# Another prologue for a graph kernel: node table in triples of blocks, edge lists in another tile, weights awaited in parts

## What is computed

```python
edge_index = jnp.stack([src, dst])
x = _layernorm(x + gat(x, edge_index, W, att), axis=-1)      # attention over the edges, 4 heads of 32
x = _layernorm(x + gnn(x, edge_index, ...), axis=-1)         # three layers of gated message passing
# gat: xh = (x @ W).reshape(-1, H, C); alpha = leaky_relu(<xh[dst], a_i> + <xh[src], a_j>)
#      softmax of alpha over the edges of one dst; out = segment_sum(xh[src] * alpha, dst)
```

## Time and profile before

| what | us |
|---|---|
| median of 3 runs (8215.47 to 8240.46) | 8240.08 |
| the profiled execution, its time | 8238.9 |
| its span, from the first to the last instruction | 8237.1 |

### The profile page before, as it was taken

The page is one execution under the profiler, slowest core; times in us unless marked ns, Lnnn a source line. Parts: engine busy times, 40 slices in busy tenths (PEclk is TensorE's granted clock), DMA queues, the critical chain, the costliest instruction groups (busy, mean ns, idle before and its releaser), DMA issues.

```text
span 8237.1 us, 134783 instructions
## 1 busy us (share of the span) xinstructions
PE 4828.4 (59%) x26657; PEld 4110.2 (50%) x26658; DVE 4929.9 (60%) x26111; ACT 1352.1 (16%) x5266; POOL 5983.1 (73%) x6316
## 2 busy tenths in 40 slices
PE   5888888888744444444464544444446444444445
PEld 4777777777644444444454444444445444444444
DVE  7777777778755555555565555555556555555555
ACT  2333333333400000000020000000011000000002
POOL 4777777777477777777757777777776777777775
PEclk6555555555655555555565555555556555555555
DMA  4444444444444444444454444444445444444443
GB/s 134 130 131 130 133 131 131 131 131 133 128 129 130 129 129 128 130 129 129 129 155 130 129 129 130 129 129 128 131 118 165 129 129 131 129 128 130 129 128 104
DMA packets 613781, 1074.03 MB, mean 130 GB/s; under 512 B 306688, under 2 KB 372128, under 8 KB 613188
## 3 DMA queue, kind: packets, MB, share of 16 engines
q0 software_dynamic: 300288, 820.39, 34.8%
q1 hardware_dynamic: 306836, 247.80, 10.1%
q10 hardware_dynamic: 6356, 3.20, 0.2%
HBM read 1025.37 MB, written 45.47 MB: 130 GB/s over the span
## 4 chain that ended last, share of the span: by engine, by line
POOL 46%; issue 22%; PE 11%; DMA 9%; DVE 8%; DVEq 2%; POOLq 1%; ACT 1%; SPq 0%; ACTq 0%
POOL G L687 46%; DMA G<-mp_rows,idx 5%; PE ps L1742 3%; DMA G<-gat_rows,idx 3%; PE ps L1642 3%; DVE junk L1454 2%; PE ps L1604 1%; PE ps L1639 1%; PE ps L1631 1%; DVEq L1065 1%; PE ps L1694 0%; PE ps L1695 0%; DVE selw L1463 0%; DVE sel L1073 0%; POOLq L684 0%
## 5 line engine op out<-in xcount | busy, mean ns | idle before, releaser
L687 POOL DMA_INDIRECT G<-mp_rows,idx x4692 | 4450.8, 949 | 1564.2 <-issue 1383.9
L1742 PE MATMUL ps<-selw,G 128*128 128x32 f32 x9384 | 2216.6, 400 | 590.3 <-DVE selw L1463 581.2
L1742 PEld LDWEIGHTS ps<-selw,G 128*128 128x128 f32 x9384 | 2088.8, 328 | 871.8 <-issue 761.2
L1443 DVE TENSOR_TENSOR pen<-ps,G 128x512 f32<-128x512 f32 x1173 | 810.9, 691 | 2733.8 <-DMA G<-mp_rows,idx 2730.1
L1732 PE MATMUL ps<-awin,ring 96*128 96x128 bf16 x4692 | 712.6, 307 | 2327.6 <-DVE ring L1428 2324.8
L687 POOL DMA_INDIRECT G<-gat_rows,idx x1564 | 1492.4, 954 | 519.5 <-issue 483.5
L1732 PEld LDWEIGHTS ps<-awin,ring 96*128 96x128 bf16 x4692 | 408.4, 131 | 2478.8 <-DVE ring L1428 2476.7
L892 ACT ACTIVATE gate<-logit,params 128x4 f32<-128x4 f32 x1173 | 348.6, 297 | 5344.4 <-DVE junk L1454 5241.0
L1454 DVE SCALAR_TENSOR_TENSOR junk<-pen,ps 128x128 f32<-128x128 f32 x4692 | 1057.5, 278 | 0.1
L1428 DVE TENSOR_TENSOR ring<-ring,ps 96x512 bf16<-96x512 bf16 x1173 | 793.7, 677 | 42.5 <-DMA ring<-rel_dst 42.5
L1642 PE MATMUL ps<-sel,weighted 128*128 128x32 f32 x3128 | 748.8, 404 | 0.0
(11 more groups left out here) (200 smaller groups left out, 4740.8 us busy)
## 6 DMA issues: line engine op xcount, KB each, us to landing
ring<-rel_dst SPq DMA_DIRECT2D x294, 384.0 KB
G<-mp_rows,idx POOLq DMA_INDIRECT x4692
ring<-rel_dst SPq DMA_DIRECT2D x98, 512.0 KB
awin<-mp_dst_rows SPq DMA_DIRECT2D x1173, 24.0 KB
G<-gat_rows,idx POOLq DMA_INDIRECT x1564
mp_rows<-acc SPq DMA_DIRECT2D x36, 512.0 KB, 2.9
mp_dst_rows<-acc SPq DMA_DIRECT2D x36, 384.0 KB, 5.3
gat_rows<-ring SPq DMA_DIRECT2D x50, 128.0 KB, 1.9
```

The costliest lines, as they stand in the source:

```text
L687: pool.indirect_dma_start(out=G[:, u, width * t:width * (t + 1)], out_offset=None, in_=table, in_offset=bass.IndirectOffsetOnAxis(ap=idx[: ...
L1443: v.tensor_tensor(pen[:, off % 2, :].rearrange("p (t c) -> p t c", t=T), PS[off % 2][:, :].rearrange("p (t c) -> p t c", t=T), Grows[:, of ...
L1742: i = mm(PS[2 + off % 2][:, 0:W], Grows[:, off % U, t, 0:D], selw[:, off % 4, W * t:W * t + W], start=(t == 0), stop=(t == T - 1))
```

## The change

The prologue is reordered, and nothing of the loops over the edges is changed apart from waits at their starts.

- The edge tiles move from `acc` and `mh` to `xT` (`rel16` to `G`). VectorE no longer fills them; GpSimd fills only the pad columns of the last two rows. The first 96 rows of each list are loaded without a wait, and dst and src have a semaphore each.
- W0 and the attention columns (two DMAs in place of eight) are loaded behind dst, with the semaphore `w0_loaded`. The large weights (`wraw`, now in `weighted`) come behind the edges with `wraw_loaded`; the other parameters are loaded by SyncE after the first eight groups of the attention stage (`load_params`). The weight transposes other than W0's follow the table.
- The table is made in 17 triples of blocks in straight-line code. x is transposed from where it was loaded, three blocks into one PSUM bank, and copied with one ScalarE instruction (`table_x`); it isn't saved in `xT`. The rows of triples 0 to 5, 8, 11 and 14 are written by ScalarE, the others by VectorE after its edge chain. There are 17 table stores and three of `gat_si`.
- TensorE transposes the edge columns between the triples (at j = 4 and j = 7). PREP_MORE now lies ahead of the eight conversions, and three constants behind the table.
- The masked maximum masks only the pad columns.

```diff
@@ tiles
-        dstI = acc[0:QP, 0, 0:QW].bitcast(I32)
-        srcI = acc[0:QP, 0, QW:2 * QW].bitcast(I32)
+        dstF = xT[0:QP, 0:QW]
+        srcF = xT[0:QP, QW:2 * QW]
+        relF = xT[0:QP, 2 * QW:3 * QW]
+        dstI, srcI = dstF.bitcast(I32), srcF.bitcast(I32)
+        rel16 = G[0:QP, 0, 0:QW // 2].bitcast(BF16)
@@ SyncE
-            sp.wait_ge(pads_filled, 2)
+            for tile, lst, loaded in edges:
+                sp.dma_start(tile[0:QS, :], lst[0:QS * QW].rearrange("(q e) -> q e", e=QW)).then_inc(loaded, 16)
+                if lst is dst:
+                    sp.dma_start(rhs0[:, 0:D], W0).then_inc(w0_loaded, 16)
...
+            sp.wait_ge(pads_filled, 3)
...
+            for j in range(3):
+                store_table(j)
             sp.wait_ge(prep, PREP_REL)
...
             gat_body(0)
+            load_params()
             with sp.Fori(1, NG // U - 1) as turn:
@@ GpSimd
+            nc.gpsimd.memset(dstI[QS:QP, QC:QW], PADDST).then_inc(pads_filled, 1)
+            pool.wait_ge(pads_filled, 2)
+            nc.gpsimd.memset(srcI[QS:QP, QC:QW], 0).then_inc(pads_filled, 1)
...
             pool.wait_ge(prep, PREP_MORE)
-            pool.wait_ge(rel_stored, 32)
             nc.gpsimd.memset(acc[:, :, :], 0.0).then_inc(acc_cleared, 1)
             nc.gpsimd.memset(mh[:, :], -BIG).then_inc(acc_cleared, 1)
@@ ScalarE
+            act.wait_ge(weightsT_ps, 1)
+            nc.scalar.copy(WT[:, :], PS[0][:, 0:D]).then_inc(weightsT_kept, 1)
+            def table_x(j):
+                n = len(triple(j)) * NB
+                if j >= 2:
+                    act.wait_ge(t0_ps, j - 1)
+                act.wait_ge(xT_ps, j + 1)
+                nc.scalar.copy(xcols[:, j % 2, 0:n], xT_bank(j)[:, 0:n]).then_inc(xT_blk, 1)
...
+            for j in range(1, NTB + 1):
+                if j < NTB:
+                    table_x(j)
+                if not by_dve(j - 1):
+                    table_rows(j - 1)
@@ VectorE
-            v.memset(dstI, PADDST).then_inc(pads_filled, 1)
-            v.memset(srcI, 0).then_inc(pads_filled, 1)
...
+            pads = dstF[QS:QP, QC:QW]
+            then(v.scalar_tensor_tensor(pads, pads, float(N), pads, ALU.is_lt, ALU.mult))
+            then(v.tensor_reduce(moreF[0:QP, :], dst_g, mybir.AxisListType.X, ALU.max))
+            then(v.tensor_tensor(moreF[0:QP, :], moreF[0:QP, :], baseF[0:QP, :], ALU.subtract))
+            then(v.tensor_single_scalar(moreI[0:QP, 0, :], moreF[0:QP, :], 0.0, ALU.max))
+            then(v.tensor_single_scalar(moreI[0:QP, 1, :], moreI[0:QP, 0, :], 5, ALU.arith_shift_right))
+            assert done[0] == PREP_MORE
...
+            for j in filter(by_dve, range(NTB)):
+                n = len(triple(j))
+                tbl_free(dve, j)
+                dve.wait_ge(t0_ps, j + 1)
+                v.tensor_copy(tbl[:, j % 4, 0:n, D:2 * D].rearrange("n b (w h) -> n b w h", h=H),
+                              out_bank(j)[:, :, D:D + H].unsqueeze(2).to_broadcast([NB, n, W, H])).then_inc(tbl_dve, 1)
+                v.tensor_copy(tbl[:, j % 4, 0:n, 0:D], out_bank(j)[:, :, 0:D]).then_inc(tbl_dve, 1)
+                v.tensor_copy(si_all[:, TB * j:TB * j + n, :], out_bank(j)[:, :, D + H:TO]).then_inc(tbl_dve, 1)
@@ TensorE
+            pe.wait_ge(w0_loaded, 48)
+            tr(PS[0][:, 0:D], rhs0[:, 0:D], ident[:, :]).then_inc(weightsT_ps, 1)
...
+            def table_gat(j):
+                pe.wait_ge(xT_blk, j + 1)
+                if j >= 2:
+                    tbl_kept(pe, j - 2)
+                for n in range(len(triple(j))):
+                    i = mm(out_bank(j)[:, n, :], xcols[:, j % 2, NB * n:NB * n + NB], rhs0[:, :], start=True, stop=True)
+                i.then_inc(t0_ps, 1)
...
+            for j in range(1, NTB + 1):
+                if j < NTB:
+                    table_turn(j)
+                table_gat(j - 1)
+                if j in (4, 7):
+                    edge_columns((4, 7).index(j))
```

More of the change, by code:

```diff
@@ L458, in a_split, with triple, xT_bank, out_bank @@
             return a_bank(q)[:, 0:n * D].rearrange("p (b d) -> p b d", b=n)
+        def triple(j):
+            return range(TB * j, min(TB * j + TB, NBLK))
+        def xT_bank(j):
+            return PS[1 + j % 2]
+        def out_bank(j):
+            n = len(triple(j))
+            return PS[3 * (j % 2)][:, 0:n * TO].rearrange("p (b c) -> p b c", b=n)
+        def triples_out(u):
+            return len(range(u, NTB, 4))
+        def by_dve(j):
+            return j >= ACTTB and j % 3 != 2
+        def tbl_kept(eng, j):
+            sem = tbl_dve if by_dve(j) else tbl_act
+            eng.wait_ge(sem, 3 * sum(by_dve(m) == by_dve(j) for m in range(j + 1)))
+        def tbl_free(eng, j):
+            if j >= 4:
+                eng.wait_ge(tbl_out[j % 4], 16 * (j // 4))
         block = ctx.enter_context(nc.Block())
@@ L498, in col @@
             def col(ap):
                 return ap.rearrange("(p o) -> p o", o=1)
[L501 to L519, removed]
@@ new lines, in _ @@
+            edges = ((dstI, dst, dst_loaded), (srcI, src, src_loaded))
+            for tile, lst, loaded in edges:
+                sp.dma_start(tile[0:QS, :], lst[0:QS * QW].rearrange("(q e) -> q e", e=QW)).then_inc(loaded, 16)
+                if lst is dst:
+                    sp.dma_start(rhs0[:, 0:D], W0).then_inc(w0_loaded, 16)
+                    with nc.allow_non_contiguous_dma(reason="columns of small weights"):
+                        for ij, lo in ((0, C), (1, 0)):
+                            sp.dma_start(acol[:, ij:ij + 1], att[0, :, lo:lo + C].rearrange(
+                                "h (c o) -> h c o", o=1)).then_inc(w0_loaded, 16)
@@ new lines, in _ @@
+            sp.wait_ge(pads_filled, 3)
+            for tile, lst, loaded in edges:
+                sp.dma_start(tile[QS:QF, :], lst[QS * QW:QF * QW].rearrange("(q e) -> q e", e=QW)).then_inc(loaded, 16)
+                sp.dma_start(tile[QF:QF + 1, 0:QC], lst[QF * QW:E].rearrange("(q e) -> q e", q=1)).then_inc(loaded, 16)
+            with nc.allow_non_contiguous_dma(reason="weights of three layers side by side"):
+                sp.dma_start(wraw[:, :, 0:2 * D], linA_w.rearrange("l k c -> k l c")).then_inc(wraw_loaded, 16)
+                sp.dma_start(wraw[:, :, 2 * D:4 * D], lin_w.rearrange("l k c -> k l c")).then_inc(wraw_loaded, 16)
+                sp.dma_start(fwraw, final_w).then_inc(wraw_loaded, 16)
@@ L540, in _ @@
-            sp.wait_ge(prep, PREP_MORE)
[L541 to L546, removed]
+            for j in range(3, 7):
+                store_table(j)
+            sp.wait_ge(counts_stored, 16)
+            sp.dma_start(base_sb[:, :], BASE).then_inc(counts_loaded, 16)
+            sp.wait_ge(prep, PREP_MORE)
@@ L547, in _ @@
+            sp.wait_ge(counts_loaded, 32)
             sp.wait_ge(rel_stored, 32)
-            sp.wait_ge(si_out, 16 * NT)
+            sp.wait_ge(si_out, 16 * len(SIB))
+            for u in range(4):
+                sp.wait_ge(tbl_out[u], 16 * triples_out(u))
             sp_regs = [sp.alloc_register(f"sp_base{n}") for n in range(U)]
@@ L774, in _ @@
                 copy_idx(0, off)
+            for l in range(L):
+                act.wait_ge(weightsT_ps, l + 2)
+                nc.scalar.copy(params[:, l, C_LP:C_LP + 4 * D], PS[1 + l][:, :]).then_inc(weightsT_kept, 1)
+            act.wait_ge(weightsT_ps, L + 2)
+            nc.scalar.copy(fwT[:, :], PS[0][:, 0:D]).then_inc(weightsT_kept, 1)
             def gat_pen(k0, off, done=gat):
@@ L1052, in _ @@
             dve.wait_ge(more_copied, 1)
-            v.tensor_reduce(shift[32:33, :], R[32:33, 0, 0:NG], mybir.AxisListType.X, ALU.add).then_inc(more_copied, 1)
+            v.tensor_reduce(shift[32:33, :], counts, mybir.AxisListType.X, ALU.add).then_inc(more_copied, 1)
             dve.wait_ge(more_copied, 2)
```

274 lines of the change are left out of this document (137 added, 137 removed).

## The result

The changed kernel took 8200.76 us (median of 4 executions, 8189.58 to 8202.53), the kernel before 8238.49 (4 executions, 8215.47 to 8240.46): ratio 0.9952, interval 0.994 to 0.9964. A second set of runs gave 8185.74 against 8221.47, ratio 0.9958, interval 0.9941 to 0.9974. So the kernel is 36 to 38 us faster. The profiled execution of the first set took 8189.58, with a span of 8187.5 us.

The account below looks back on a forecast made before the run. GpSimd's unbroken gather issue was taken as the bound, with the prologue ahead paid in full. Moving the first gather from 105.3 to 64 gives -41.3 us: 8238.9 to 8197.6, set at 8199 as median; range 8170 to 8214.

Parts of the forecast that it names:

- The bound and the passing-on: Attention stage: GpSimd issues gathers without a stop, so moving the first gather moves the kernel's end equally, 41.3 us.
- T: Start of the attention stage's first gather, in us: 105.3 in the kernel before, predicted 64.
- Edge lists, 14: Prologue loads: both edge lists, issued from 0.8, land at about 14 us instead of 18.30; bounds 11 and 18.
- ScalarE's start, 18.5 kept: Prologue: ScalarE, busy issuing x loads, still starts its own work at 18.50 us; bounds 18 and 24.
- The pace, 1.9 us a triple: Table making: each triple of 128-node blocks takes 1.9 us, from 1.8 to 1.95 per three blocks before.
- The rival of a slow table: Table: low TensorE clock or held PSUM reads cost 12 or 13 us more; T 76, 8211 us; chance 0.22.
- two sets of edge columns: TensorE's edge-column transposes between table triples: the first done at 31 us, the second at 39.5.
- The short copy, to the end of the first clear: VectorE's 16-column SBUF copy, under GpSimd's clear of the accumulators, waits for that clear's end: 41.5 to 41.8 us.
- The stores are no limit: End of the table: a table store of 384 KB needs only 1.2 us, so stores don't set the pace.
- W0 awaited by itself, worth nothing: Prologue: W0 lands early, at about 9 us, but gains nothing before 19.8 because ScalarE is the limit.
- Parameters behind the first groups, worth nothing: Attention stage start: parameter loads of 10.2 us fit in 18.3 us of room: zero; without cover, up to 10.
- Slower by the gathers' pitch: Rival in the gather loop: at 997 ns a gather instead of 954, 25 us slower, 8265 us; chance 0.05.

Follow-up runs that it names:

- e5: Changed kernel with short copy on ScalarE, three x loads on ScalarE, two score stores, VectorE's constants ahead of its wait for the attention columns: 8173.41 us, ratio 0.9942 to kernel before.
- e6: Changed kernel with GpSimd's two clears started behind VectorE's 16-column copy instead of at PREP_MORE: T 64.3 us.
- e1: Changed kernel with the 16-column index copy moved from VectorE to ScalarE: T 63.23 us.
- e8: Kernel before with only x transposed where it was loaded, VectorE's 50 copies gone and TensorE's table steps written out: T 88.8 us against 104.2 to 105.3.
- e4: Changed kernel with the short copy on ScalarE and the second score store joined with the last, behind all table stores: T 60.3 us.
- e9: Changed kernel with TensorE waiting for the large weights too before transposing W0: T 71.05 us.
- e7: Changed kernel with the 11 small parameter loads issued ahead of the first eight groups' offsets and windows: T 70.45 us.
- e2: Changed kernel with ScalarE issuing only three x loads, SyncE the others behind the weights; short copy still on VectorE: T 66.68 us.

## Why the prediction was right, step by step

**The bound and the passing-on: right.** The prologue is paid in full, and GpSimd's loop runs at the same pitch behind it. The time, 8199 against 8200.8, is closer than its parts, and that is luck: T was 70.5 in the first profile and 65.3 in the second, where 64 was predicted, and the first set's executions of one kernel scatter by 13 to 25 us. The gain in time, 37.7 and 35.7, is fairer to hold against the 41.3 predicted. Several steps were off and partly cancelled: VectorE's rows behind the short copy began at 48.84 or 43.88, not at 41.8, and from there to T it took 21.6 and 21.4, where 22.2 was predicted, since a faster pace made up for the waits for stores.

**Edge lists, 14; measured 15.7 to 16.** They land at 15.9 (e5's wait), within the bounds. PREP_MORE came at 32.5 instead of 30.7, the clears with it.

**ScalarE's start, 18.5 kept; measured 22.15.** The prediction had the reason and 24 as a bound, and took the unchanged value. ScalarE's first copy was 3.6 late, and in the second profile it came at 24.04, just past the 24 that the prediction named as a sign of being wrong. The first six triples made up for it: VectorE's last conversion ended at 40.4, where 40.3 was predicted.

**The pace, 1.9 us a triple: too slow a figure where the clock is high.** ScalarE's rows of triples 1 to 3 are 1.2 apart, and between 58 and 61 TensorE's matmuls of successive triples are 1.15 apart at full clock (2.4 GHz); after the pause, with the clock at 0.50 between 50 and 54 (1.2 GHz), they are 2.1 apart. This is TensorE's timeline:

```profile
50.09 1.70 PE L1634 MATMUL ps<-rhs,ring 128*128 128x136 f32 x6 [10.48 <-DVE pen L1095]
52.22 1.57 PE L1634 MATMUL ps<-rhs,ring 128*128 128x136 f32 x6
...
58.25 0.96 PE L1634 MATMUL ps<-rhs,ring 128*128 128x136 f32 x6
59.40 0.93 PE L1634 MATMUL ps<-rhs,ring 128*128 128x136 f32 x6
```

The block time of the earlier trace rows was VectorE's (three instructions and a copy of x a block: it was busy for all 1.32 us from 88.00 to 89.32), not that of the chain that I named. The rival of a slow table (12 to 13 us more) did not come: the clock was low for some 5 us, at a cost of 2.4 (2.13, 2.00 and 1.71 from one triple's matmuls to the next, against 1.15), where 0.5 was allowed.

TensorE's two sets of edge columns were counted at 2.3 and 2.8 and took 2.05 each.

**The short copy, to the end of the first clear: half right.** It is held, as e6 shows (0.17 without a clear), but in three of five executions through both clears, 7 us more than priced (2 of these because the clears began later). In the other two it was those 2. The prediction read the four L1028 copies of the earlier trace rows as "the end of the clear"; the end at which a waiting copy gets in is not certain. The trace of the kernel before couldn't tell: taken singly, its first two copies (min/median/max in ns, first and last start) end with the first clear, and so they do in its second profile:

```profile
L1028 DVE TENSOR_SCALAR ring<-G x2: 10690/10728/10765, 46.0 to 46.2; 128x128 f32<-128x128 f32 x2
```

The other half, that instructions reading PSUM are not held, is right in e1, e6 and e8. The rule of the Trainium skill, "SBUF — State Buffer", section "Who interferes with whom", is stated there for VectorE's two-port modes, which a copy can enter, and frees an instruction with at most one input in SBUF outside these modes. The runs agree with both: the copy is held (2.66 to 8.40 us), the rows from PSUM are not (0.56). It doesn't say who wins when GpSimd has two clears in a row, and here it went either way.

**"The stores are no limit": wrong.** By bytes it holds (349 GB/s at 66 to 68), but 18 blocks of scores in pieces of 16 bytes stood in the same queue, and the last rows waited 3.70 us (e4: 4.4). I had priced the table stores and not looked at what lies between them.

**W0 awaited by itself, worth nothing: right** (e9). **Parameters behind the first groups, worth nothing: right** (e7), though their issue takes 5.7 us there and not 10.2.

**Slower by the gathers' pitch:** means of 945 to 954 ns in all six profiles of the faster chips; never near 980.

Of the gain of 34.8 to 38.9 in T, x turned in place gives 15.4 to 16.4 by itself (e8). The rest, the earlier lists, the clears off the end, the table ahead of the edge chain and in triples, wasn't tried part by part; how it divides stays open.

## What to carry to other kernels

Before moving a long GpSimd instruction over other work, list every VectorE copy with both operands in SBUF that can fall under it, the tiny ones above all: a copy of 0.17 us held up the table by up to 8.4. Give such a copy to ScalarE or put it ahead of the clear. When costing stores, look at the small pieces that share their queue, not only at the bytes. And when one set of loads is started earlier, look at what becomes of the others and of the engine that issues them: here ScalarE came free 4.3 us later (22.1 against 17.8).

## What the runs showed of the hardware

- A VectorE copy that waits for a GpSimd clear gets in between two clears in some executions and not in others of the same program: ends at 43.85 and at 48.81. A VectorE instruction that reads PSUM runs beside the clear at its usual duration (0.56 us in e1, 0.29 in e8).
- DMA engines fully busy moved 80 GB/s while a store in pieces of 16 bytes went through, and 349 four microseconds later with pieces of 1 KB.
- ScalarE's queue needed 10.76 us for the five loads of x when the edge loads started at 5.2, and 18.91 when they started at 0.8, with other loads moved too. ScalarE's copy of W0, whose transpose was ready at 13.2, came behind the queue at 23.45; with three loads in the queue (e2) it came at 12.69.
- The mean duration of an indirect gather differs by 1 to 2 ns between two executions of the kernel before, which over 6256 gathers is 7.8 us, most of the 10.7 between their spans.
